# Channel attention on one core: twelve of 49 tap tiles of exponentials gathered by accumulating DMAs, and TensorE's shifts issued in pairs

## The reference

```python
q = jnp.einsum('bchw,oc->bohw', x, w_q)
kmap = jnp.einsum('bchw,oc->bohw', x_pad, w_k)
vmap = jnp.einsum('bchw,oc->bohw', x_pad, w_v)
kwin = _unfold2d(kmap, K)
vwin = _unfold2d(vmap, K)
kwin = jnp.concatenate([kwin[:, :half] + rel_h, kwin[:, half:] + rel_w], axis=1)
attn = jax.nn.softmax(q[..., None] * kwin, axis=-1)
out = jnp.sum(attn * vwin, axis=-1)
```

## Time and profile before

| | us |
|---|---|
| median of three runs | 7987.79 (7983.30 to 7996.58) |
| the profiled execution | 7993.27, span 7991.6 |
| first to last shift of channel attention | 3315 to 7303 of the span |
| one band of channel attention (the seventh) | 249.28 |

### The profile page before, as it was taken

The page is one execution under the profiler, slowest core; times in us unless marked ns, Lnnn a source line. Parts: engine busy times, 40 slices in busy tenths (PEclk is TensorE's granted clock), DMA queues, the critical chain, the costliest instruction groups (busy, mean ns, idle before and its releaser), DMA issues. The chain is left out here.

```text
span 7991.6 us, 141890 instructions
## 1 busy us (share of the span) xinstructions
PE 7529.3 (94%) x55106; PEld 6489.6 (81%) x55106; DVE 5666.6 (71%) x8853; ACT 3670.7 (46%) x7040; POOL 4566.2 (57%) x2002
## 2 busy tenths in 40 slices
PE   5999998989998999599999999999999999997999
PEld 4777776879997776388888888888888888886999
DVE  5666665334443555688888888888888888896664
ACT  3655655423332332255555555555555555554222
POOL 3555552023332000388888888888888788886232
PEclk9999998999999999799999999999999999998999
DMA  3111113865557873100000000000000000002452
GB/s 142 61 58 67 60 58 122 282 161 144 144 147 194 234 210 109 29 20 23 27 18 17 20 23 27 18 18 19 24 27 18 17 20 24 27 9 93 138 164 78
DMA packets 633018, 617.21 MB, mean 77 GB/s; under 512 B 465525, under 2 KB 498421, under 8 KB 627174
## 3 DMA queue, kind: packets, MB, share of 16 engines
q1 hardware_dynamic: 581318, 483.44, 21.8%
q0 software_dynamic: 33856, 96.69, 3.3%
q10 hardware_dynamic: 17376, 30.54, 1.0%
HBM read 397.01 MB, written 193.76 MB: 74 GB/s over the span
## 5 line engine op out<-in xcount | busy, mean ns | idle before, releaser
L1909 POOL TENSOR_TENSOR e_ev<-e_se,e_v 128x2048 f32<-128x2048 f32 (+1 forms) x896 | 3307.7, 3712 | 760.6 <-ACT e_se L1847 758.1
L1847 ACT ACTIVATE e_se<-e_stage 128x512 f32<-128x512 f32 x3136 | 1867.8, 597 | 1851.4 <-PE e_stage L1679 1792.9
L1998 DVE SCALAR_TENSOR_TENSOR e_stage<-e_k,e_rl,e_qp 128x512 f32<-128x512 f32 x3136 | 2290.5, 747 | 340.7 <-ACT e_se L1847 285.7
L1686 PE MATMUL e_pe_sum<-e_ident,e_se 128*128 128x128 f32 x12544 | 1880.6, 272 | 16.5 <-ACT e_se L1847 12.3
L1686 PE MATMUL e_pv_sum<-e_ident,e_ev 128*128 128x128 f32 x12544 | 1875.4, 273 | 0.5 <-POOL e_ev L1909 0.5
L1686 PEld LDWEIGHTS e_pe_sum<-e_ident,e_se 128*128 128x128 f32 x12544 | 1550.6, 140 | 259.1 <-ACT e_es L1835 21.8
L1686 PEld LDWEIGHTS e_pv_sum<-e_ident,e_ev 128*128 128x128 f32 x12544 | 1477.2, 140 | 204.6 <-issue 203.2
L1679 PE MATMUL e_stage<-e_top,e_minus 128*128 128x512 f32 x3136 | 1507.8, 481 | 89.2 <-DVE e_stage L1998 85.6
L911 POOL DMA_DIRECT2D agg<-c_ot x384 | 334.6, 874 | 878.7 <-ACT c_ot L989 769.1
L403 POOL TENSOR_TENSOR a_pr<-a_pr,a_rden 128x480 f32<-128x480 f32 x512 | 494.1, 985 | 547.6 <-DVE a_rden L636 547.6
L1679 PEld LDWEIGHTS e_stage<-e_top,e_minus 128*128 128x128 f32 x3136 | 595.5, 190 | 143.6 <-DVE e_stage L1998 99.7
(11 more groups left out here) (175 smaller groups left out, 11567.5 us busy)
## 6 DMA issues: line engine op xcount, KB each, us to landing
qkv<-b_ot SPq DMA_DIRECT2D x120, 512.0 KB, 5.9
c_xt<-qkv SPq DMA_DIRECT2D x384, 160.0 KB, 3.8
agg<-c_ot POOLq DMA_DIRECT2D x384, 160.0 KB, 2.5
f_ws<-in_L_w_sets SPq DMA_DIRECT2D x32, 1152.0 KB, 7.9
a_xb<-in_x SPq DMA_DIRECT2D x24, 768.0 KB, 5.1
a_xr<-in_x SPq DMA_DIRECT2D x32, 512.0 KB, 3.8
x<-a_xr SPq DMA_DIRECT2D x32, 512.0 KB, 2.7
b_xc<-x SPq DMA_DIRECT2D x32, 512.0 KB, 5.8
```

Source lines behind the costliest of these rows:

```text
L1686: last = nc.tensor.matmul(acc[:, c * PART:(c + 1) * PART], lhsT=src[:, c * PART:(c + 1) * PART], rhs=ident[:], is_transpose=True, start=j ...
L1847: nc.scalar.activation(se[(t * K2 + o) % NSE][:, i], stage[:, bank_of(t, j), :], ACT.Exp)\
L1909: nc.gpsimd.tensor_tensor(split(ev[(t * NG2 + g) % NEV][:, 0:size]), split(se[(t * K2 + o) % NSE][:, i:i + size]), window(v[h], h, u, o, i ...
L1998: nc.vector.scalar_tensor_tensor(rows(stage[:, bank_of(t, j), :]), win, rl[:, h, o:o + 1], rows(qp[:]), ALU.add, ALU.mult).then_inc(multip ...
```

## The change

Four things change in `channel_attention`, and nothing outside it.

- **Four gathered places.** Two new buffers `acc` (tiles take turns) hold four taps each. The exponentials of row 0, places 0 to 3, are written there instead of into `se`. For rows 1, 2 and 3 (`GATHERED`), POOL issues one DMA each that adds the row's places 0 to 3 out of `se` onto `acc` in SBUF: 128 x 2048 floats, 1 MB. POOL waits for the earlier DMA to land before it issues the next.
- **Fewer sums on PE.** The exponential sums of these 16 taps go. In their place PE adds the four places of `acc` at taps 42, 44, 46 and 48, so a tile has 37 exponential sums (`NES`) instead of 49.
- **Shifts in pairs.** PE's `step` does work at even taps alone, for taps j and j + 1: weighted sum of j, both shifts, both exponential sums, weighted sum of j + 1. Projections keep their taps.
- **Waits.** A row of `se` that was gathered is written again when its DMA has landed; the others when their sums are made.

Cut to its core:

```diff
+        acc = [sb(f"acc{u}", [PART, ROW_PARTS[0][1], TPX]) for u in range(2)]
...
+        GATHERED = (1, 2, 3)
+        NACC = ROW_PARTS[0][1]
+        DIRECT = [j for j in range(NTAP) if j % K2 >= NACC or j // K2 not in (0, *GATHERED)]
+        NES = len(DIRECT) + NACC
+        ACC_AT = (42, 44, 46, 48)
...
+        def exps(t, j, taps=None):
+            o, i = divmod(j, K2)
+            buf = acc[t % 2] if o == 0 and i < NACC else se[(t * K2 + o) % NSE]
+            return buf[:, i] if taps is None else buf[:, i:i + taps]
...
+            def sum_gathered(n, t, i):
+                if i == 0:
+                    pe.wait_ge(gathered, gathers(n, t, K2))
+                add_up(pe_sum, acc[t % 2][:, i], False, False).then_inc(e_summed, 1)
...
+            def exponential_of(n, t, j, first):
+                if (t * NTAP + j >= E_LAG or not first) and before(t, j, E_LAG)[1] in DIRECT:
+                    sum_exponential(n, *before(t, j, E_LAG), first=first)
+                if j in ACC_AT:
+                    sum_gathered(n, t, ACC_AT.index(j))
...
             def step(n, t, j, first=False, final=False):
                 h, u = tile_of(t)
-                late = j == V_LAG
-                if not late and (t * NTAP + j >= V_LAG or not first):
-                    sum_weighted(n, *before(t, j, V_LAG), first=first)
-                shift(n, t, j)
-                if t * NTAP + j >= E_LAG or not first:
-                    sum_exponential(n, *before(t, j, E_LAG), first=first)
-                if late:
-                    sum_weighted(n, t, 0, first=first)
+                taps = [i for i in (j, j + 1) if i < NTAP] if j % 2 == 0 else []
+                late = [i for i in taps if i == V_LAG]
+                for i in taps[:1]:
+                    if i not in late:
+                        weighted_of(n, t, i, first)
+                for i in taps:
+                    shift(n, t, i)
+                for i in taps:
+                    exponential_of(n, t, i, first)
+                for i in taps:
+                    if i in late or i != taps[0]:
+                        weighted_of(n, t, i, first)
...
+            def gather(n, t, o):
+                if o == GATHERED[0]:
+                    pool.wait_ge(weighted, tiles(n, t, NG2, 1))
+                else:
+                    pool.wait_ge(gathered, gathers(n, t, o - 1))
+                pool.wait_ge(exp_done, tiles(n, t, NTAP, o * K2 + NACC))
+                flat = lambda x: x.rearrange("p i n -> p (i n)")
+                pool.dma_start(flat(acc[t % 2][:]), flat(se[(t * K2 + o) % NSE][:, 0:NACC]), accum_op=ALU.add).then_inc(gathered, 16)
...
                     for g in range(NG2):
+                        if g % 2 == 0 and g // 2 in GATHERED:
+                            gather(n, t, g // 2)
                         weigh(n, t, g, first=n == 0)
```

More of the change, by code:

```diff
@@ L1450, in channel_attention @@
         weighted = sem("weighted")
+        gathered = sem("gathered")
         e_summed = sem("e_summed")
@@ L1571, in bank_lag, with sums_made, gathers, part_of @@
             return 2 if t * NTAP + j in (1, TPB * NTAP - 1) else NST
+        def exps(t, j, taps=None):
+            o, i = divmod(j, K2)
+            buf = acc[t % 2] if o == 0 and i < NACC else se[(t * K2 + o) % NSE]
+            return buf[:, i] if taps is None else buf[:, i:i + taps]
+        def sums_made(n, t, j):
+            return tiles(n, t, NES, sum(d <= j for d in DIRECT) + sum(a < j + E_LAG for a in ACC_AT))
+        def gathers(n, t, o):
+            return 16 * tiles(n, t, len(GATHERED), sum(r <= o for r in GATHERED))
+        def part_of(j):
+            return group_of(j) % len(ROW_PARTS)
         def group_of(j):
@@ L1830, in take_e_sums @@
             def take_e_sums(n, t):
-                act.wait_ge(e_summed, tiles(n, t, NTAP, NTAP))
+                act.wait_ge(e_summed, tiles(n, t, NES, NES))
                 if t > 0 or n:
@@ L1840, in exponential @@
                 start, size = ROW_PARTS[g % 2]
-                if i == start and (t * NTAP + j >= NSE * K2 or not first):
-                    t0, j0 = before(t, j, NSE * K2)
-                    act.wait_ge(e_summed, tiles(n, t0, NTAP, j0 + size))
-                    act.wait_ge(weighted, tiles(n, t0, NG2, group_of(j0) + 1))
+                if j == 0 and (t >= 2 or not first):
+                    act.wait_ge(e_summed, tiles(n, t - 2, NES, NES))
+                elif i == start and j:
+                    lag = NSE * K2
+                    if part_of(j) == 0 and before(t, j, lag)[1] == 0:
+                        lag *= 2
+                    if t * NTAP + j >= lag or not first:
+                        t0, j0 = before(t, j, lag)
+                        if part_of(j) == 0 and j0 // K2 in GATHERED:
+                            act.wait_ge(gathered, gathers(n, t0, j0 // K2))
+                        else:
+                            act.wait_ge(e_summed, sums_made(n, t0, j0 + size - 1))
+                        act.wait_ge(weighted, tiles(n, t0, NG2, group_of(j0) + 1))
                 act.wait_ge(shifted, tiles(n, t, NTAP, j + 1))
-                nc.scalar.activation(se[(t * K2 + o) % NSE][:, i], stage[:, bank_of(t, j), :], ACT.Exp)\
-                    .then_inc(exp_done, 1)
+                nc.scalar.activation(exps(t, j), stage[:, bank_of(t, j), :], ACT.Exp).then_inc(exp_done, 1)
             def open_extreme(H, s):
```

21 lines of the change are left out of this document (12 added, 9 removed).

## The result

The changed kernel takes 8131.16 us (median of four runs, 8118.86 to 8136.18) beside 7992.18 for the kernel before (7983.30 to 7999.19, four runs): 139 us more, a ratio of 1.017 [1.0155, 1.0186]. The forecast was 8004 in a range of 7900 to 8100, so the time lies above the range, on the side that held the larger chance.

A forecast was written before the change was run, and what follows sets the result against it. PE (busy 94%) was taken to lead, with DVE setting the pace in some stretches. Odd tiles +0.26 us, even +0.66, pairing -0.2 a tile: 1.04 a band, about +17 in 16 bands, giving 8004 us, range 7900 to 8100.

The forecast's parts named there:

- Pairing itself: Ten pairs a tile where PE is full: each hides 0.02 us of a shift, so 0.2 us a tile won.
- Taps 28 to 41: nothing: Odd tiles, taps 28 to 41: the change neither wins nor loses time there.
- The working for taps 12 and 13 of odd tiles: Shift 13 waits for its multiply behind the division until 15.45 us, holding back 3.75 us of PE work; shift 14 at 19.2.
- DVE is busy for 26.23 of 26.23 us in tile 0's middle: Profile reading for tile 0, taps 12 to 27: DVE full there, so PE's relief was not counted.
- From there to tap 28 DVE is full, and I give nothing: Even tiles, from DVE's neighbour step to tap 28: no time won or lost, after 1.1 us won before it.
- Odd tiles, taps 0 to 11: Start of odd tiles: earlier reciprocals bring tap 12's shift to 14.1 us instead of 15.1, 1.0 us won.
- 1.76 is lost: Taps 42 to 48, where PE has no gap: four returned exponential sums at 0.44 us add 1.76 us a tile.
- The four taps 16 to 19 take about 3.3 us: Sign that the forecast is right: these taps of odd tiles, without exponential sums, take about 3.3 us.
- the bank loop of a pair: Odd tiles, taps 16 to 19: three banks looping through shift, exponential and multiply hold a pair to 1.67 us; PE needs 1.34.
- first rival: PE's relief counts wherever DVE shows any gap: 87 us faster, 7901; sign: light taps at 0.67 us each; chance 0.20.
- POOL at nothing: POOL's three DMAs a tile stay hidden, landing within 7.4 us of multiplying: cost nothing.
- pairs cost more than counted: Third rival: PE stands still at odd taps' shifts with finished work queued; one more us a tile, 64 us, 8070; chance 0.14.

## Why the prediction was wrong

**The step that failed** is the one called "Pairing itself", with its companion in "Taps 28 to 41: nothing". It priced a pair as 0.02 us won, from the time that a shift is busy. Pairs alone cost 144 us, 2.2 us a tile, and 43 us stand for those at taps 28 to 48, where the step expected 0.2 us a tile (13 us) of gain. Even the 0.02 is not there: a pair that waits for nothing lasts 2.21 us (4969.19 to 4971.40 in the change), two single taps 2 x 1.11. The working for taps 12 and 13 of odd tiles had the mechanism in full: the odd tap's shift waits for its multiply and holds back what is queued behind it. I applied it at this one place, where a division is visible between the multiplies, and not at the other 23 pairs. There DVE has such a step between two multiplies often too: a neighbour step, a running maximum. Not each of them costs, as the table of the pairs shows.

How small the slack of a pair is follows from rows that I had. Exponential 26 starts 0.52 us after shift 26 and exponential 27 is 0.60 behind it. So the bank for multiply 29 is free 1.12 us after the pair's start. If DVE is at hand, that multiply ends 0.75 later, at 1.87, and shift 29 is due at 2.21 + 0.23 = 2.44. The slack is 0.57 us; a step of DVE's running maximum takes 0.66, and a neighbour step of tile 0 0.60 to 1.44. That working is mine, after the fact; what the runs show is the waits (0.60 us at tap 29 above) and their sum.

**A second step failed with it.** "DVE is busy for 26.23 of 26.23 us in tile 0's middle" was read as proof that DVE bounds this stretch, so that an idle PE costs nothing there. The first half holds for tile 0. In the kernel with pairs alone its stretch reads:

```profile
4893.25:4921.33 28.08, 23.74 (x160) 19.04 (x161) 28.08 (x34) 10.33 (x18) 18.15 (x6) 1.00 0.08 28
```

DVE is full again, and by the starts of its own instructions it is no slower: from multiply 13 to multiply 28 it takes 24.82 us before and 24.81 with the pairs, without a gap in either. The stretch is longer because it ends with a shift of PE, and this shift comes later behind its multiply. Multiply 28 and shift 28 before, and with the pairs:

```profile
4855.51 0.77 DVE L1998 SCALAR_TENSOR_TENSOR e_stage<-e_k,e_rl,e_qp 128x512 f32<-128x512 f32 x1
...
4856.43 0.48 PE L1679 MATMUL e_stage<-e_top,e_minus 128*128 128x512 f32 x1
```

```profile
4918.64 0.77 DVE L2059 SCALAR_TENSOR_TENSOR e_stage<-e_k,e_rl,e_qp 128x512 f32<-128x512 f32 x1
...
4921.33 0.48 PE L1703 MATMUL e_stage<-e_top,e_minus 128*128 128x512 f32 x1
```

PE is 2.69 us behind the multiply, and was 0.92 behind it before. What PE stood still for did not slow DVE down here, but it left PE with work that it has to do where DVE no longer sets the pace. The kernel with pairs at taps 0 to 27 but for 12 and 13 shows that bill: past tap 28 it has no pairs, its PE is full there (17.26 of 17.26 us), and of the 1.8 us that taps 12 to 27 cost, tile 0 gets only 1.0 back. In tile 2 even the first half fails: from multiply 13 to 28 DVE takes 20.67 us without a gap before and 21.89 with 1.17 us of gaps with the pairs. With gathering alone and no pairs, tile 2's middle fell from 22.86 to 21.86 us, and again DVE's own time did not change (20.62); what changed is that shift 28 came 0.79 us behind its multiply in place of 1.73. "From there to tap 28 DVE is full, and I give nothing" was wrong on both sides, because it took PE's delay at the end of the stretch for nothing.

**What held.** Odd tiles, taps 0 to 11: 1.0 won, measured 0.80; even tiles 1.1, measured 0.83 and 1.04. From an odd tile's first shift, shift 12 was put at 14.1 and came at 14.3, shift 14 at 19.2 and 19.3, shift 16 at 21.4 and 21.5, shift 20 at 24.7 and 24.6. Shift 28 was put at 33.9 and came at 34.4, the first of the missing half microseconds. Even tiles: shift 8 at 9.7, measured 9.68 in tile 0 and 9.48 in tile 2. The end: 9.51 forecast, 9.49 in the row above; "1.76 is lost" measured 1.74. The reciprocals' idle time shrank as forecast, from 51.4 to 31.8 us. Two signs came out otherwise: PE's idle time ahead of its shifts grew to 6.2 us a tile (398.7 / 64) and not to 3 or 4, and DVE stayed full in tile 0's middle but not in tile 2's (22.89 of 24.05 us).

**Right number, wrong reason.** "The four taps 16 to 19 take about 3.3 us" came to 3.08, but the bank loop of a pair is not why: tap by tap, with gathering alone, they take 3.05. Three of them follow each other at 0.67 us each, and at the fourth PE waits for DVE. My text named light taps at 0.67 as a sign for the first rival. In the kernel with gathering alone they are there, and odd tiles' taps 12 to 19 win 1.46 us, where my sum had 0.4; the end of the tile takes it back.

**POOL at nothing** held. The landing was put between 6.3 and 12.0 and taken nearer to 6.3; it is 7.2, just under the 7.4 that cost nothing. By an estimate from the formula of the Trainium skill (DMA: Bandwidth & Descriptors, section Anatomy of one DMA) 1 MB would land in 4.4 us and twice that in 6.8; the trace is nearest to the second, which fits a destination that is read too, and no run here separates that from a plain copy of this size.

**The rivals.** The third, "pairs cost more than counted", is what happened. PE's idle time ahead of the shifts of odd taps is 318 us, and was 41 before, though the loss sits at fewer places than "all over" says. Its chance was 0.14 and its price one us a tile, 8070; the price was about two. PE's relief (first rival) shows in one place: added to the pairs, gathering takes 5 us off (143.8 to 139), where alone it costs 35. Why the two overlap by 40 us, most of it at taps 0 to 19, was not tried; a PE that stands still at odd taps loses less if it has less to do, which is an argument and not a measurement. Open as well is a part of the misses with rows 4 and 5: the even tiles' gains and the ends explain their sum only roughly.

## What to carry to other kernels

On an engine that works through its instructions in order, as PE's order here is fixed by the program, do not put an instruction that may wait ahead of work that is ready: in a loop of shift, exponential and multiply over three banks the pairing of two shifts cost 2.2 us a tile, though no instruction was added. Take work off an engine only in stretches in which it, and not its neighbour, sets the pace, and look where the rest comes back: here most of the relief fell where it won little, and all the returns fell where PE had no gap. A full engine X in a stretch does not make its neighbour's delay free: it can be worked off only where the neighbour has time left behind the stretch. And a stretch that is cut at the neighbour's instructions grows with that delay, while X stays full; whether X itself got slower shows in the starts of X's own instructions.

## What was unexpected in the hardware

**The granted clock dips where PE has been given less to do.** Most stretches stand at 1.00, the 2.4 GHz level; within a dip it is 0.5, 1.2 GHz, so a stretch of 17.79 us with one dip has a mean of 0.90. Over the attention stage, its start left out, where the clock is still low from the layer before, the kernel before has 2 dips, the one with pairs alone 1, the changed one 13. Ten of these start at tap 13 of an even tile, where PE had just stood still for 1.7 us in two waits (0.95 ahead of shift 12 and 0.76 ahead of shift 13, medians of tile 0). With the division one tap later the second wait is 0.16, no dip starts at tap 13, and 3 are left in all. The kernel that gathers rows 3, 4 and 5 in all tiles has 16, ten of them at tap 34 or 35 of tile 1, behind the 1.90 us for which PE stands still there. In that kernel, taps 28 to 41 of tile 1 take 16.83 us without a dip and 17.6 to 17.8 with one, so ten dips make some 9 us. Leaving tile 1 as it was took these ten away, left 8 in all, and gave 8 us (-15.3 beside -6.9). How much of that is the clock and how much the returns saved was not tried; by the stretches the clock's share alone would be as large.

**An adding DMA beside POOL's multiplications lengthens their records more than their time.** Groups of POOL by shape, of the change and of the same kernel without its DMAs:

```profile
L1963 POOL TENSOR_TENSOR e_ev<-e_se,e_v 128x2048 f32<-128x2048 f32 x384 | 1708.5, 4449 | 111.7 <-ACT e_se L1902 111.7
```

```profile
L1963 POOL TENSOR_TENSOR e_ev<-e_se,e_v 128x2048 f32<-128x2048 f32 x384 | 1616.8, 4210 | 638.7 <-ACT e_se L1902 493.8 <-PE e_pv_sum L1710 141.6
```

A mean of 4449 ns beside 4210, and 4218 in the earlier trace rows. But by their starts the second multiplication of a gathered row still follows the first after 4.18 us (4.19 before), and both together end after 7.66 us in place of 7.40: 0.27 us a row, hidden here. The Trainium skill (SBUF — State Buffer, section Who interferes with whom) says that a DMA never contends with a compute engine; the run without DMAs (7.37 us for the two) shows that these DMAs do lengthen POOL's work a little. Whether the transfer or its issue on POOL does so was not tried. Loads that meet the DMAs are slower too: `e_xb` of 704 and 608 KB land in 8.6 and 7.0 us, in the kernel before in 7.0 and 6.2, and in the change without its DMAs in 6.9 and 6.1.
